# Opening by deadline, one list for query and value products, expert weights merged on two engines

## The reference, cut to what matters

```python
xn = layernorm(x)
# graph network, with agg = segment_sum(h[src], dst)
h = prelu(xn @ lin_W.T + lin_b)
for l in range(2):
    h = h + agg(h)
    h = prelu(h @ W1[l].T + b1[l]) @ W2[l].T + b2[l]
    h = relu(batchnorm(h))
# attention, 8 heads of 64
q, k, v = split(xn @ w_qkv)
q = softmax(q, over a head's 64) / 8
k = softmax(k, over the 1250 nodes)
context = k.T @ (v / 1250)                      # per head
mix = layernorm((context, q) @ w_out + b_out) * ln_scale
x = x + h + mix
# feed-forward block
y = layernorm(x)
g = mean over nodes of (relu(y @ gfc1.T + gfc1_b) @ gfc2.T + gfc2_b)   # 8 numbers
W1m = W1 + sum_e g[e] * tv_W1[e];  b1m = b1 + g @ tv_b1
W2m = W2 + sum_e g[e] * tv_W2[e];  b2m = b2 + g @ tv_b2
out = relu(y @ W1m.T + b1m) @ W2m.T + b2m
x = x + layernorm(y + out) * lng + lnb
# lng, lnb: sums over the eight experts' rows, known before g
```

## Time and profile before

| | |
|---|---|
| median of 3 runs | 597.02 us (596.97 to 597.75) |
| profiled execution, its own time | 595.26 us |
| its span, first to last instruction | 593.4 us |
| mean granted TensorE clock | 0.918 |
| busy: PE, DVE, ACT, POOL | 497.3, 363.6, 229.4, 196.7 us |
| DMA | 27.45 MB, mean 46 GB/s |

### The profile page before, as it was taken

The page is one execution under the profiler, slowest core; times in us unless marked ns, Lnnn a source line. Parts: engine busy times, 40 slices in busy tenths (PEclk is TensorE's granted clock), DMA queues, the critical chain, the costliest instruction groups (busy, mean ns, idle before and its releaser), DMA issues.

```text
span 593.4 us, 11554 instructions
## 1 busy us (share of the span) xinstructions
PE 497.3 (84%) x3899; PEld 392.1 (66%) x3899; DVE 363.6 (61%) x737; ACT 229.4 (39%) x516; POOL 196.7 (33%) x159
## 2 busy tenths in 40 slices
PE   1890799999889889999999967999999699866750
PEld 0780678766546756679988956898889488535530
DVE  3659678758888376464276443214763654499794
ACT  2552322273413332224346365212553677203431
POOL 4683210044510210025955500003451000465873
PEclk9995879999879999999999979999999589887985
DMA  8402010010020010020000200000202940000022
GB/s 238 149 1 72 4 68 2 1 43 29 1 72 1 21 53 1 1 75 0 0 1 1 71 0 3 2 0 7 116 0 71 390 181 2 0 2 0 0 80 92
DMA packets 5006, 27.45 MB, mean 46 GB/s; under 512 B 796, under 2 KB 921, under 8 KB 3304
## 3 DMA queue, kind: packets, MB, share of 16 engines
q1 hardware_dynamic: 4660, 25.90, 12.5%
q10 hardware_dynamic: 308, 1.02, 0.6%
HBM read 24.36 MB, written 2.56 MB: 45 GB/s over the span
## 4 chain that ended last, share of the span: by engine, by line
PE 61%; DVE 20%; ACT 7%; POOL 6%; issue 4%; DMA 1%; ACTq 0%; DVEq 0%; SPq 0%; POOLq 0%
PE ps L435 36%; PE ps L576 14%; PE ps L422 4%; DVE stage L1359 4%; PE ps L486 2%; POOL late L1449 2%; DVE stat L1042 2%; PE ps L476 1%; POOL r L1510 1%; PE ps L419 1%; DVE r L1123 1%; ACT r L875 1%; DMA x<-in_x 1%; DVE qsum L1172 1%; DVE r L1166 1%
## 5 line engine op out<-in xcount | busy, mean ns | idle before, releaser
L435 PE MATMUL ps<-r,wslot 128*128 128x250 f16 x840 | 103.2, 286 | 10.0 <-DVE wslot L1021 5.1
L435 PE MATMUL ps<-late,wslot 128*128 x960 | 104.8, 269 | 0.8 <-ACT ohs L849 0.8
L1458 POOL TENSOR_TENSOR wslot<-stage,wslot 128x2048 f16<-128x2048 f32 x9 | 36.8, 4085 | 207.1 <-ACT wslot L714 133.5
L435 PEld LDWEIGHTS ps<-r,wslot 128*128 128x128 f16 x840 | 86.8, 104 | 24.0 <-DVE wslot L1021 5.9
L435 PEld LDWEIGHTS ps<-late,wslot 128*128 128x128 f16 x960 | 92.2, 97 | 13.1 <-issue 3.3
L576 PE MATMUL ps<-late,r 125*128 (+1 forms) x800 | 90.0, 274 | 4.9 <-issue 3.7
L576 PEld LDWEIGHTS ps<-late,r 125*128 125x128 f16 x800 | 78.4, 99 | 14.7 <-issue 5.9
L435 PE MATMUL ps<-wslot,r 128*125 128x512 f16 x300 | 74.1, 402 | 8.0 <-DVE r L1402 4.9
L1021 DVE SCALAR_TENSOR_TENSOR late<-ps,late 128x250 f32 (+2 forms) x60 | 29.9, 507 | 64.9 <-ACT late L882 55.3
L435 PEld LDWEIGHTS ps<-wslot,r 128*125 128x125 f16 (+1 forms) x300 | 42.1, 145 | 33.2 <-issue 14.2
L721 ACT ACTIVATE late<-ps 125x500 f16<-125x500 f32 (+1 forms) x25 | 14.7, 588 | 93.7 <-PE ps L422 93.7
(11 more groups left out here) (158 smaller groups left out, 732.3 us busy)
## 6 DMA issues: line engine op xcount, KB each, us to landing
late<-in_tv SPq DMA_DIRECT2D x2, 4096.0 KB, 17.6
out<-r SPq DMA_DIRECT2D x10, 250.0 KB
stage<-in_w_up SPq DMA_DIRECT2D x2, 1024.0 KB, 4.9
stage<-in_w_down SPq DMA_DIRECT2D x2, 1024.0 KB, 4.8
x<-in_x SPq DMA_DIRECT2D x3, 448.0 KB
stage<-in_w_lin SPq DMA_DIRECT2D x1, 1024.0 KB, 10.7
stage<-in_w_k SPq DMA_DIRECT2D x1, 1024.0 KB, 5.0
stage<-in_w_q SPq DMA_DIRECT2D x1, 1024.0 KB, 4.7
```

Source lines behind the costliest of these rows:

```text
L435: last = nc.tensor.matmul(out, stat_(hs, b), mov(hm, b), start=start and n == 0, stop=stop and n == 3 * blocks - 1)
L1458: nc.gpsimd.tensor_tensor(wslot[:, i % SLOTS, 1].rearrange("p k n -> p (k n)"), stage[:, :], wslot[:, i % SLOTS, 0].rearrange("p k n -> p ...
```

## The change

Opening. All pairs of x load from SP, pair 0, then the weight, then the rest. The first two pairs are normalized on ScalarE, and GpSimd normalizes the last three (`POOL_NORM = 2`). VectorE makes the first quarter of the weight's high half. TensorE flips the next pair behind block m = 2 of a chunk, in place of ahead of the chunk; ScalarE's blocks 0 and 1, root, high halves, blocks 2 and 3 follow in that order. Nine comparisons become three instructions. The high half of "k" and the window search come after the halves of the last pair, and the search's product stands within the last chunk.

Query and value. One list `QV`: q0 to q6, then v0 q7 v1 q8 v2 q9 v3 and v4 to v9. Two key tiles are transposed after each of q2 to q6. For a value tile ScalarE takes the high half and then the count bank; VectorE writes the one-hots and then takes the low half. ScalarE's half of weight "out" comes after the first value tile, and GpSimd's work on "out" ahead of its ten products.

Ending. The experts' norm rows are loaded and summed ahead of the gate stage, and GpSimd adds ln_b within it. g comes from a product of sums over partitions. TensorE adds 4, 3, 4 and 3 experts of the four weight parts (`PE_SHARE`), VectorE the others. b2 is split into two rows of f16 and enters the last product as one more matmul per tile; the ten additions on GpSimd are gone. ScalarE's halves stand between hidden blocks.

```diff
+POOL_NORM = 2
+PE_SHARE = (4, 3, 4, 3)
+Q_FIRST, KN_LAG = 7, 2
+QV = [("q", _t) for _t in range(Q_FIRST)]
+for _t in range(T):
+    QV += [("v", _t)] + ([("q", Q_FIRST + _t)] if Q_FIRST + _t < T else [])
...
@@ SyncE
             load_x(sp, 0)
             sp.dma_start(stage[:, :], dram["w_lin"]).then_inc(got_w, 16)
+            load_x(sp, 1)
             load_x(sp, 2)
             sp.dma_start(cols[:, :], dram["cols"]).then_inc(got_cols, 16)
+            load_x(sp, 3)
             load_x(sp, 4)
...
+            sp.wait_ge(tmp_free, KB + KB * J * L)
+            sp.dma_start(tvrow, dram["tv_rows"]).then_inc(got_tvrow, 16)
             sp.wait_ge(full["t"], before("t", "gate"))
-            sp.dma_start(tvrow, dram["tv_rows"]).then_inc(got_tvrow, 16)
...
@@ TensorE
+            flip_pair(0)
+            for j in range(J):
+                wait_done(pe, "x", "xn", 2 * j + 2)
+                for m in range(KB):
+                    pe.wait_ge(lin_low, m + 1)
+                    product("lin", KB * j + m, m, weight("lin"), m, xn_t, slice(j * CH, (j + 1) * CH))
+                    if m == 2 and j + 1 < J:
+                        flip_pair(j + 1)
+                    if m == 2 and j + 1 == J:
+                        pe.wait_ge(firsts, 1)
...
+            for i, (kind, t) in enumerate(QV):
+                if (kind, t) == ("v", 0):
+                    wait_weight(pe, "v")
+                natural_tile("qv", xn_t, weight(kind), t, i)
+                if kind == "q" and KN_LAG <= t < Q_FIRST:
                     pe.wait_ge(k_exp, KB)
-                    flip_tile_to_nat("x", "kn", k_t, t - 2)
+                    for u in (2 * (t - KN_LAG), 2 * (t - KN_LAG) + 1):
+                        flip_tile_to_nat("x", "kn", k_t, u)
+                if kind == "v" and t:
                     windows("v", (t - 1) // 2, (t - 1) % 2, 2)
...
+            def merge_on_pe(bank_, part, share):
+                for k in range(PE_EXPERTS - share, PE_EXPERTS):
+                    pe.wait_ge(diag_ready, k + 1)
+                    last = nc.tensor.matmul(bank_, g_diag[:, k, :], part(E - PE_EXPERTS + k), start=(k == PE_EXPERTS - share),
+                                            stop=(k == PE_EXPERTS - 1))
+                last.then_inc(pe_merged, 1)
...
+            merge_w1(6, 0)
             pe.wait_ge(g_vec, 1)
             nc.tensor.matmul(ps[0:P, 7, :], grow[:, :], tvrow[:, 2, :], start=True, stop=True).then_inc(b2_sum, 1)
+            merge_w1(5, 1)
             for m in range(FB):
                 pe.wait_ge(wm_split, m + 1)
                 for j in range(J):
                     product("ffn1", J * m + j, (J * m + j) % 4, w1m, m, x2_t, slice(j * CH, (j + 1) * CH))
+                if m == 0:
+                    merge_w2(4, 0)
+                    merge_w2(6, 1)
             pe.wait_ge(wm_split, FB + 2)
+            pe.wait_ge(b2_ready, 2)
...
@@ ScalarE
+            for j in range(J):
+                lin_blocks(j, (0, 1))
+                if j + 2 < HT:
+                    deviations(2 * j + 4, 2 * j + 6, TURN["xn"] + j + 2, scaled=1)
+                if j + 1 < HT:
+                    for t in (2 * j + 2, 2 * j + 3):
+                        high_tile_t("xn", xn_t, t)
+                lin_blocks(j, (2, 3))
...
+                    nc.scalar.activation(v_nat[:, 0, t, :], bank("n", i % 2)[0:P, :], ACT.Copy, scale=1 / S_W).then_inc(v_high, 1)
+                    windows("v", t // 2, t % 2, 2)
+                    if t == 0:
+                        split_weight("out")
...
+            high_w1(0)
             act.wait_ge(b1_done, 1)
+            for i in range(FB * J):
                 hidden(i)
+                if i == J - 2:
+                    high_w1(1)
+                if i in (J - 1, J + 1):
+                    high_w2(int(i > J))
...
@@ VectorE
-            then(nc.vector.tensor_scalar(src_tile, ints[:, 0, :], float(P), None, ALU.is_ge))
-            for h in range(2, T):
-                then(nc.vector.scalar_tensor_tensor(src_tile, ints[:, 0, :], float(P * h), src_tile, ALU.is_ge, ALU.add))
+            then(nc.vector.tensor_scalar(tile_i, ints[:, 0, :], 1 / P, -0.496, ALU.mult, ALU.add))
+            then(nc.vector.scalar_tensor_tensor(src_tile, tile_i, -float(P), ints[:, 0, :], ALU.mult, ALU.add))
+            then(nc.vector.scalar_tensor_tensor(src_tile, src_tile, float(P), tile_i, ALU.is_ge, ALU.add))
...
+            merge(w1_part(wm32[:, 0, :], 1), lambda e: w1_part(tv[:, 0, e, :], 1), E - PE_SHARE[1])
+            add_pe_part(w1_part(wm32[:, 0, :], 1), ps[:, 5, :].rearrange("p (k f) -> p k f", k=KB), 2)
+            dve.wait_ge(b2_sum, 1)
...
+            low_w1(1)
...
+            merge_w2(0)
+            add_pe_part(wm32[:, 1, half(0)], ps[:, 4, :], FB + 1)
+            merge_w2(1)
+            low_w2(0)
+            add_pe_part(wm32[:, 1, half(1)], ps[:, 6, :], FB + 2)
+            low_w2(1)
...
@@ GpSimd
-            for g in range(HT):
+            for g in range(POOL_NORM, HT):
                 normalize(g)
             nc.gpsimd.memset(ctx16[:, :, :, :], 0.0).then_inc(consts, 1)
-            for name in ("k", "q", "v"):
+            for name in ("k", "q", "v", "out"):
                 split_weight(name)
...
+            pool.wait_ge(b2_added, 1)
+            nc.gpsimd.tensor_scalar(b2_row[0:2 * LOW_ROW, :], b2_row[0:2 * LOW_ROW, :], S_B, 1.0, ALU.mult, ALU.mult
+                                    ).then_inc(b2_split, 1)
...
+            pool.wait_ge(b2_ready, 2)
             for i in range(FB * J):
                 low_hidden(i)
-                if i % 2 and HT + 1 + i // 2 < T:
-                    add_b2(HT + 1 + i // 2)
```

356 lines of the change are left out of this document (181 added, 175 removed).

## The result

The changed kernel takes 569.04 us (median of four executions, 568.28 to 574.7) where the kernel before takes 597.0: the ratio is 0.9575, with a 95% interval of 0.9542 to 0.9608, so it is faster, by 4.3%. Forecast were 564 and a range of 551 to 579. The profiled execution took 569.8 us with a span of 568.0; the span before was 593.4, so 25.4 us went out of it, where the sum of the prediction said 33.4.

The account below looks back on a forecast made before the run. TensorE was taken as the bound on average, with 61% of the chain. Terms -17 - 5 + 0.6 - 12 = -33.4 took the profiled 595.3 to 561.9; plus 1.76 for the median, 564 us, range 551 to 579.

Parts of the forecast that it names:

- the bank: End of the opening: the first count bank would come at 55.5 to 57.5 us instead of 74.27.
- Opening: Up to the first count bank: earlier x and reordered queues save 17 us, bounds 20 and 11.
- moves as a block: From 74.3 to 118.2 us and other stages with kept code: TensorE is busy throughout, so time won earlier stays won.
- List: Query and value in one list: ideal gain 13 us, 5 after GpSimd and ScalarE stops; bounds 11 and 0.
- rival 1: GpSimd's port takes more: opening -11, list 0, ending -7.5, gate 0.6, giving 579 us; chance 0.24.
- Rows of the layer norm: Ahead of the gate stage: moving the rows' products and additions there loses 0.6 us, bounds 0 and 1.5.
- Ending: From the gate to the end: shared merges and b2 as a matmul save 12 us, bounds 16 and 6.
- the bias product hides behind VectorE: Last product: the added matmul, 0.22 us a tile, costs nothing; without VectorE's cover 2.2 us.
- one SBUF operand is safe: VectorE beside GpSimd: instructions with one SBUF operand (statistics, splits out of PSUM) show no stretching.
- Rival 2: No stall worth naming, clock at 2.4 GHz: opening -20, list -11, ending -16, giving 550 us; chance 0.16.
- Rival 3: ScalarE becomes the opening's bound: waits at 8 us a chunk give opening -9, 572 us; chance 0.07.
- Rival 4: Slower than before: GpSimd's 50 us beside two-operand VectorE work falls wholly on the path, 599 us; chance 0.03.

Follow-up runs that it names:

- undo_opening: The changed kernel with only its opening put back as it was before; 585.25 us.
- after_again: The changed kernel, nothing altered, measured and profiled a second time as base for later runs; 569.5 us.
- qsub_late: The changed kernel with GpSimd's subtraction of q's weight waiting until the third window's one-hots are made; 570.3 us.
- undo_list: The changed kernel with only query and value put back: ten query tiles, then ten value tiles, softmax products before the out weight's split; 570.93 us.
- soft_small: The changed kernel with GpSimd's ten softmax products cut from 512 columns to 8, so later stages compute on other numbers; 567.73 us.
- undo_ending: The changed kernel with only the ending put back: layer-norm rows after the gate, W1 merges on VectorE alone, b2 added by GpSimd; 579.59 us.
- warm: The changed kernel with 28 needless matmuls in TensorE's wait ahead of the last product; 565.59 us.

## Why the prediction was right, and where it was not

The time, 569.0, lies in the range and 5 us above the forecast; in the profiled execution the sum was 8.0 us too good (33.4 against 25.4). The difference is luck: the forecast added the 1.8 us by which the median before lay above its profiled execution, and the median after lies 0.8 below its own. Of the signs that the prediction named, the list (78.9, not 70 to 77) and the bank (58.4, not 55.5 to 57.5) fell outside, and two signs of being wrong came true: the clock of the last stretch is 0.74, and the k stage does not move as a block. By its own steps:

**Opening, -17, bounds -20 and -11: right, 15.9 in the trace to the first bank; 12 to 16 in all by undo_opening, with the k stage's loss in it.** x landed at 5.10 (estimate 5.5). The chunks, forecast at 12.1, 20.3, 27.2, 33.6 and 41.9, came at 11.7, 20.7, 27.7, 34.1 and 43.3. The stop of 4 us at the window search was there, 4.04; TensorE waited 0.8 for it, not 2.5. What was missing is that the wait ahead of chunk 4 (3.06) would be followed by half clock: 5.68 instead of 4.01 for its three blocks.

**The k stage "moves as a block": wrong, +1.8 in this profile, +3.3 in after_again, and at least +1.4 in every kernel with the new opening.** This is the one assumption without a term: that TensorE was busy 43.89 of 43.90 us there was read as proof that what is won ahead of it stays won, and says nothing of what the feeding engines will meet. The code is the same, but the opening brought its start forward by 16 us, and the split of q's weight on GpSimd, which hangs on VectorE's cast of k, by 11 (from 68.7 to 57.8): the subtraction that used to end before the first bank now starts just ahead of it. undo_opening has 44.0 again. What the earlier trace rows priced at 4 us was held against the window search alone; the next such subtraction in GpSimd's queue was not laid beside VectorE's queue. Moving that subtraction away (qsub_late) took the wait of 3.25 but did not bring 44.0 back, so how the loss divides between the stop and the half clock around it stays open.

**List, -5, bounds -11 and 0: mechanism right, size wrong, 1.5 in the trace, 0.8 by undo_list's.** The ideal start of the value tiles, 23.3 us after the first query tile, was 23.7. Off it went 2 for ScalarE's split (1.7 measured), 4.5 for the port and 1.5 for up0 and the clock. The ten products cost 2.6 (soft_small). The term that was too small is the last: the scaling of up0 makes one L1059 2.40 long, TensorE waits 1.24, and the clock falls for the bank and the tile behind it (12 passes in 4.46 and not 2.78): 4.3 in all where 1.5 was taken. With that and the port's term too large by 1.9, the three terms come to 8.6 against 8.0; nearly 3 of the 3.5 us missed are in no term. The largest piece is the last bank, 3.1 us with a wait of 0.8 for ScalarE in it, as long as in the kernel before, where the sum had 1.0. So rival 1's list (0) is nearer than the forecast's, but only in part for the reason it gave.

**Rows of the layer norm, +0.6: 0.3 in the trace**, within what stages of equal code differ by.

**Ending, -12, bounds -16 and -6: right.** In the first profile, with the cut at the first bias product, 14.8 were won before it and 4.7 lost after it, 10.1 in all, and 10.1 by undo_ending's median; by stages against after_again it is 12.4. Working the two queues out gave 32.2 for the way to the last product; it is 32.2 to the bias product. The allowance of 1.3 for the clock in front wasn't needed. The 1.5 for the clock behind it is what one slow tile costs (39.2 against warm's 37.9: 1.3) and was too small where two are slow (41.4: 3.5); the "up to 3.4 more" is the price of two (14 passes of 0.22 us more each would be 3.1). Two of eight profiles have two, six have one. With the clock held (warm) the stage is 37.9, 0.5 over before, so the step "the bias product hides behind VectorE" stands.

Sum of the misses in the first profile: 1.1 opening, 1.8 k stage, 3.5 list, 1.9 ending, less 0.3: 8.0. Half clock behind a wait cost 6.9 us at three places of this profile (1.7 in chunk 4, 1.7 in the list, 3.5 at the end), where the sum had 1.5 at the end, a share of 1.5 in the list and nothing in the opening.

The Trainium skill (GPSIMD Engine Reference, section 8, Key points), cited for its rule on VectorE instructions with two SBUF inputs or in a two-port mode, holds here for the comparisons and the merges, which have two inputs in SBUF. The instructions stopped longest, though, have one input in SBUF and a handful of numbers (25 in the cast of 4.04 us, 16 in the earlier trace rows); whether they run in a two-port mode the profile does not show. Instructions that read PSUM kept their time beside the products (L1069 and L1229, 0.68 and 0.67 us at 147.9 and 148.5). My own line in the prediction, that one SBUF operand is safe, is wrong for these small ones.

Rival 2 (no stall, clock at 2.4 GHz) was right for the merges alone: 8 in 3.26 us free of GpSimd. Rival 3 is out, but not by the distance of the chunks, which is 7.9 us on average and so its own 8: its -9 did not follow from that distance, and the opening gave 15.9. What speaks against it is that ScalarE is busy only 43% to 71% of a chunk's time and TensorE waits for VectorE ahead of chunks 1, 3 and 4. Rival 4 is out: of the 50 us of GpSimd's work beside VectorE, waits and stage differences show about 6.4 on the path (0.8 search, 1.8 k stage, 2.6 products, 1.2 up0).

## What to carry to other kernels

When one stage is pulled forward, list what other engines' queues hold at its new start, above all the long SBUF-to-SBUF instructions of GpSimd: a stage whose code is unchanged still changes if its neighbour in time does. Price a wait of TensorE in front of a burst not at its length alone: here waits of 3.06 to 3.5 us were followed by some 3 to 6 us of work at half clock. If there is nothing useful to put there, a few needless matmuls in that one place can pay (3.9 us in the median here, 1.3 to 3.5 in their stage); three more such places did not pay here, and why is open. Judge a small step by its stage in the trace and in more than one profile, since one half-clock stretch more or less moves a stage or the total by as much.
